# A conditioned transformer block on one core: inputs loaded earlier, weights split in halves, a new order of the tiles, and filler products ahead of the first tile's transposes

## The reference

```
def _tc_rmsnorm(x, t, gw, gb, bw, bb):
    g = (t @ gw.T + gb)[:, None, :]
    b = (t @ bw.T + bb)[:, None, :]
    inv_rms = jax.lax.rsqrt(jnp.mean(x * x, axis=-1, keepdims=True) + EPS)
    return g * x * inv_rms + b
...
x = x + _attention(_tc_rmsnorm(x, t, g1w, g1b, b1w, b1b), Wq, Wk, Wv, Wo)   # 16 heads of 16
return x + _swiglu(_tc_rmsnorm(x, t, g2w, g2b, b2w, b2b), gate_w, hid_w, out_w)   # 1024 hidden
```

## Time and profile before

| | |
|---|---|
| median of 3 runs | 944.69 us (942.25 to 944.82) |
| the profiled execution | 942.75 us, its span 940.5 us |
| mean granted clock of TensorE | 0.987 |
| busy in the span | PE 898.8 us, DVE 624.5, ACT 552.3, POOL 493.3 |

### The profile page before, as it was taken

The page is one execution under the profiler, slowest core; times in us unless marked ns, Lnnn a source line. Parts: engine busy times, 40 slices in busy tenths (PEclk is TensorE's granted clock), DMA queues, the critical chain, the costliest instruction groups (busy, mean ns, idle before and its releaser), DMA issues.

```text
span 940.5 us, 24138 instructions
## 1 busy us (share of the span) xinstructions
PE 898.8 (96%) x8988; PEld 771.4 (82%) x8988; DVE 624.5 (66%) x1067; ACT 552.3 (59%) x1255; POOL 493.3 (52%) x409
## 2 busy tenths in 40 slices
PE   5668999999999999999999999999999999999998
PEld 3456888978888898888888888888888888888887
DVE  3637668486866848677584867758476775857642
ACT  4456657565665756566575656657575665655541
POOL 4554637364563746456373644737365472735433
PEclk9879999999999999999999999999999999999999
DMA  5300102020110101011020101102010110200000
GB/s 194 102 24 23 35 25 57 2 56 22 45 34 22 56 0 56 22 45 34 19 59 0 56 22 45 34 5 73 0 54 24 45 34 0 56 0 23 2 23 23
DMA packets 25595, 34.06 MB, mean 36 GB/s; under 512 B 3296, under 2 KB 20896, under 8 KB 25440
## 3 DMA queue, kind: packets, MB, share of 16 engines
q1 hardware_dynamic: 25344, 33.59, 11.5%
q10 hardware_dynamic: 224, 0.10, 0.0%
HBM read 25.27 MB, written 8.42 MB: 36 GB/s over the span
## 4 chain that ended last, share of the span: by engine, by line
PE 88%; DVE 4%; ACT 4%; issue 3%; DMA 1%; POOL 0%; ACTq 0%; SPq 0%; DVEq 0%
PE ps L1084 9%; PE ps L1086 9%; PE ps L1085 9%; PE ps L1220 7%; PE ps L1226 7%; PE ps L1221 6%; PE ps L1236 6%; PE ps L1239 6%; PE ps L1237 6%; PE ps L1192 5%; PE ps L1207 4%; PE ps L1112 4%; PE ps L1113 3%; PE ps L1115 3%; PE ps L1182 2%
## 5 line engine op out<-in xcount | busy, mean ns | idle before, releaser
L293 POOL TENSOR_TENSOR h_lo<-h,h_hi 128x512 fp32r<-128x512 f32 x128 | 164.1, 1291 | 178.7 <-ACT h_hi L522 178.7
L299 POOL TENSOR_TENSOR probs<-probs,recip 128x512 f32<-128x512 f32 x128 | 131.8, 1045 | 48.6 <-DVE recip L829 47.1
L840 DVE SCALAR_TENSOR_TENSOR shared<-shared,ps 128x512 f32<-128x512 f32 x128 | 86.8, 678 | 97.1 <-ACT shared L517 97.1
L1084 PE MATMUL ps<-out_w_hi,h_hi 128*128 128x256 f32 x512 | 144.9, 283 | 0.0
L1086 PE MATMUL ps<-out_w_hi,h_lo 128*128 128x256 f32 x512 | 144.7, 283 | 0.0
L1085 PE MATMUL ps<-out_w_lo,h_hi 128*128 128x256 f32 x512 | 144.2, 282 | 0.0
L1220 PE MATMUL ps<-xn_hi,gate_w_hi 128*128 128x512 f32 x256 | 106.2, 415 | 2.5 <-ACT xn_hi L488 2.0
L847 DVE SCALAR_TENSOR_TENSOR h<-shared,ps 128x512 f32<-128x512 f32 x128 | 87.4, 683 | 28.9 <-PE ps L1239 23.5
L517 ACT ACTIVATE shared<-ps 128x512 f32<-128x512 f32 x128 | 76.1, 595 | 51.6 <-PE ps L1226 51.6
L532 ACT COPY probsT<-ps 128x512 f32<-128x512 f32 x128 | 69.2, 590 | 63.1 <-PE ps L1192 63.1
L1236 PE MATMUL ps<-xn_hi,hid_w_hi 128*128 128x512 f32 x256 | 106.2, 415 | 0.0
(11 more groups left out here) (92 smaller groups left out, 2008.0 us busy)
## 6 DMA issues: line engine op xcount, KB each, us to landing
x_in<-in_x SPq DMA_DIRECT2D x16, 512.0 KB, 3.4
xT_in<-in_xT SPq DMA_DIRECT2D x16, 512.0 KB, 3.3
out<-result SPq DMA_DIRECT2D x15, 512.0 KB, 3.0
inv_all<-inv_rows SPq DMA_DIRECT2D x15, 256.0 KB, 3.9
shared<-in_attT SPq DMA_DIRECT2D x1, 1024.0 KB, 7.8
shared<-in_gateT SPq DMA_DIRECT2D x1, 1024.0 KB, 9.7
shared<-in_hidT SPq DMA_DIRECT2D x1, 1024.0 KB, 4.8
shared<-in_outT SPq DMA_DIRECT2D x1, 1024.0 KB, 5.8
```

The costliest lines, as they stand in the source:

```text
L293: nc.gpsimd.tensor_tensor(h_lo[:, j % KEPT, :], h[:, j % 2, :], h_hi[:, j % KEPT, :].bitcast(F32), ALU.subtract).then_inc(h_lo_done, 1)
L299: nc.gpsimd.tensor_tensor(own, own, recip[:, p % TOGETHER, :].unsqueeze(2).to_broadcast([P, SEQS, L]), ALU.mult).then_inc(divided, 1)
L1084: nc.tensor.matmul(dst, a_hi, b_hi, start=first, stop=False, skip_group_check=skip)
```

## The change

The change has five parts.

1. *Early input.* SP loads tile 1's input right after the weights have been issued and, in later tiles, at the start of the iteration. x_res is loaded from memory by a transfer of its own; `keep_input` on ScalarE is gone.
2. *Head.* PE spreads the factors before the first gains. VectorE writes the scaled first tile into PSUM (`PAIR + 2` and `PAIR + 3`) and does the whole first norm of tile 0 from there (`whole_norm1`), both channel halves, instead of a half on VectorE and a half on ScalarE.
3. *Weights in halves.* Gate, hidden and out weights are split in two pieces each; `w_split` counts to 8 instead of 5.
4. *New orders* for all tiles on all engines. In the first tile ScalarE also makes the second keys and queries, VectorE the first queries.
5. *Fillers.* In the first tile each `transpose_probs` is preceded by four filler products into its own bank, once `shift` has used the scores there.

```diff
@@ SP
+            sp.wait_ge(ms1_done, 1)
+            sp.dma_start(x_in[:, :, :], x_t[1]).then_inc(x_loaded, 16)
+            sp.wait_ge(scaled1, 1)
+            sp.dma_start(xT_in[:, :, :], xT[1]).then_inc(xT_loaded, 16)
+            sp.dma_start(x_res[:, :, :], x_t[0]).then_inc(x_res_loaded, 16)
...
+                elif attend:
+                    if ahead:
+                        sp.wait_ge(ms1_done, t + 1)
+                        sp.dma_start(x_in[:, :, :], x_t[t + 1]).then_inc(x_loaded, 16)
+                        sp.wait_ge(scaled1, t + 1)
+                        sp.dma_start(xT_in[:, :, :], xT[t + 1]).then_inc(xT_loaded, 16)
+                    sp.wait_ge(sum_done, t)
+                    sp.dma_start(x_res[:, :, :], x_t[t]).then_inc(x_res_loaded, 16)
+                    if finish:
+                        sp.wait_ge(result_done, 2 * (t - 1))
+                        sp.dma_start(out_t[t - 2], result[:, :, :]).then_inc(stored, 16)
+                    if ahead:
+                        next_factors(t)
@@ GpSimd, first tile
+                next_inverse(t)
+                low_gate_weights(0)
+                low_gate_weights(1)
                 divide(t, 0)
-                low_hid_weights()
-                next_inverse(t)
                 divide(t, 1)
+                scale_rows(t + 1)
                 divide(t, 2)
                 divide(t, 3)
+                low_hid_weights(0)
                 divide(t, 4)
+                low_norm1(t + 1, 0)
+                low_norm1(t + 1, 1)
                 divide(t, 5)
                 divide(t, 6)
-                scale_rows(t + 1)
                 divide(t, 7)
-                low_norm1(t + 1, 0)
-                low_norm1(t + 1, 1)
-                low_out_weights()
+                low_hid_weights(1)
+                low_out_weights(0)
+                low_out_weights(1)
@@ VectorE, head
-                nc.vector.tensor_tensor(xn1[:, :, :], xT_in[:, :, :],
+                nc.vector.tensor_tensor(ps[:, PAIR + 2:PAIR + 4, :], xT_in[:, :, :],
...
+            def whole_norm1():
+                for c in range(CH):
+                    scaled = ps[:, PAIR + 2 + c, :].rearrange("p (b q) -> p b q", q=L)
+                    last = nc.vector.tensor_tensor(scaled, scaled, of_sequences(0, c, 0), ALU.mult)
+                last.then_inc(gained1, 1)
+                dve.wait_ge(gained1, 1)
+                for c in range(CH):
+                    nc.vector.tensor_tensor(xn1[:, c, :].rearrange("p (b q) -> p b q", q=L),
+                                            ps[:, PAIR + 2 + c, :].rearrange("p (b q) -> p b q", q=L),
+                                            of_sequences(1, c, 0), ALU.add).then_inc((xn1_first, xn1_second)[c], 1)
@@ VectorE, steady tile, middle
                 silu(u, 4)
+                first_norm1(t + 1)
                 hidden(u, 4)
                 row_maxima(t, 4)
...
-                first_norm1(t + 1)
@@ PE
             def transpose_probs(t, p):
+                if alone(t):
+                    pe.wait_ge(shift_done, p + 1)
+                    keep_clock_up(FILL_STEP, bank_of(t, p))
                 pe.wait_ge(divided, PAIRS * t + p + 1)
...
+            pe.wait_ge(consts_in, 16)
+            spread_factors()
             pe.wait_ge(mod_in, 2 * 16)
             gains_and_shifts(0)
-            pe.wait_ge(consts_in, 16)
-            spread_factors()
@@ PE, steady tile, first half after the change
                 gate(u, 0)
                 scores(t, 0)
                 hid(u, 0)
                 gate(u, 1)
                 hid(u, 1)
                 gate(u, 2)
+                hid(u, 2)
                 down(u, 0)
-                hid(u, 2)
                 gate(u, 3)
+                hid(u, 3)
+                down(u, 1)
+                gate(u, 4)
                 transpose_probs(t, 0)
                 transpose_probs(t, 1)
-                hid(u, 3)
-                gate(u, 4)
                 transpose_probs(t, 2)
                 transpose_probs(t, 3)
                 hid(u, 4)
                 scores(t, 1)
                 values_probs(t, 0)
                 gate(u, 5)
...
```

More of the change, by code:

```diff
@@ L439, in _, with high_weights @@
             act.wait_ge(table_loaded, 1)
-            def high_weights(n, landed, count, hi, piece):
-                act.wait_ge(landed, count)
-                nc.scalar.copy(hi, raw[:, piece, :]).then_inc(w_hi_done, 1)
+            def high_weights(landed, hi, piece, half):
+                act.wait_ge(landed, 16)
+                nc.scalar.copy(hi, raw[:, piece, half * HID:(half + 1) * HID]).then_inc(w_hi_done, 1)
             def mean_squares(u, src, ready, counts, trash, read, ms, ms_done):
@@ L490, in first_keys @@
             def first_keys(u):
+                if alone(u):
+                    act.wait_ge(consts_in, 16)
                 act.wait_ge(k_mm, CH * u + 1)
@@ L539, in _, with high_att_weights, high_gate_weights, other_keys @@
             squares1(0)
-            act.wait_ge(att_w_in, 16)
-            for part in range(2):
+            def high_att_weights(part):
+                act.wait_ge(att_w_in, 16)
                 nc.scalar.copy(att_w_hi[:, 2 * part:2 * part + 2, :, :].rearrange("p m c n -> p (m c n)"),
                                raw[:, 0, part * HID:(part + 1) * HID]).then_inc(w_hi_done, 1)
-            act.wait_ge(consts_in, 16)
-            act.wait_ge(mod_done, 2 * CH)
-            second_norm1(0)
+            high_att_weights(0)
             for c in range(CH):
                 high_norm1(0, c)
[L549 to L557, removed]
+            high_att_weights(1)
+            def high_gate_weights(half):
+                high_weights(gate_w_in, gate_w_hi[:, half, :], 1, half)
+            def other_keys(u):
+                act.wait_ge(k_mm, CH)
+                for head in range(2):
+                    last = nc.scalar.activation(keys[:, 1, :, head, :],
+                                                ps[:, k_bank(u, 1), :].rearrange("p (b q) -> p b q", q=L), ACT.Copy,
+                                                scale=head_mask[:, head:head + 1])
+                last.then_inc(keys1_done, 1)
+            def other_queries(u):
+                act.wait_ge(q_mm, CH)
+                nc.scalar.copy(queries[:, 1, :], ps[:, q_bank(u, 1), :]).then_inc(queries1_done, 1)
+            def high_hid_weights(half):
+                high_weights(hid_w_in, hid_w_hi[:, half, :], 0, half)
+            def high_out_weights(half):
+                high_weights(out_w_in, out_w_hi[:, KEPT * half:KEPT * half + KEPT, :].rearrange("p j n -> p (j n)"),
+                             1, half)
             def scale_second(t):
@@ L946, in steady_tile @@
                 row_maxima(t, 0)
+                shift(t, 0)
+                hidden(u, 0)
                 row_maxima(t, 1)
+                shift(t, 1)
+                silu(u, 1)
                 row_maxima(t, 2)
-                hidden(u, 0)
-                shift(t, 0)
-                silu(u, 1)
-                shift(t, 1)
                 hidden(u, 1)
-                reciprocals(t, 0)
                 row_maxima(t, 3)
+                shift(t, 2)
                 silu(u, 2)
-                reciprocals(t, 1)
-                shift(t, 2)
                 hidden(u, 2)
                 shift(t, 3)
+                reciprocals(t, 0)
+                reciprocals(t, 1)
                 reciprocals(t, 2)
@@ L1021, in last_tile @@
                 shift(t, 4)
+                hidden(u, 4)
                 shift(t, 5)
@@ L1024, in last_tile @@
                 reciprocals(t, 4)
-                silu(u, 4)
                 row_maxima(t, 7)
-                hidden(u, 4)
+                shift(t, 6)
+                low_attention(t, 0)
+                silu(u, 5)
+                shift(t, 7)
                 reciprocals(t, 5)
-                shift(t, 6)
-                shift(t, 7)
-                low_attention(t, 0)
                 reciprocals(t, 6)
-                silu(u, 5)
                 reciprocals(t, 7)
@@ L1127, in project_q @@
                     pe.wait_ge(xn1_lo_done, CH)
-                    wait(pe, q_act_done, c)
+                    wait(pe, queries0_done, c)
                 else:
@@ L1413, in after_last @@
                 gate(u, 2)
-                down(u, 0)
                 hid(u, 2, False)
                 gate(u, 3)
+                down(u, 0)
                 hid(u, 3, False)
@@ L1424, in after_last @@
                 gate(u, 6)
+                down(u, 3)
                 hid(u, 6, False)
-                down(u, 3)
                 gate(u, 7)
```

312 lines of the change are left out of this document (156 added, 156 removed).

## The result

The changed kernel takes 969.76 us (median of 4 runs, 967.97 to 971.37); the kernel before, run beside it, 943.73 (942.25 to 944.82). The ratio is 1.0278, with a 95% interval of 1.0266 to 1.0291: slower by 26 us, where 968 us was forecast.

What follows compares the result with a forecast made beforehand. PE was taken to bound the kernel, with 88% of the chain and almost no slack in steady tiles. 942.75 - 11 (start) + 30.8 (hold) + 5.5 (clock) = 968 us; own range 955 to 980, 8-in-10 range 942 to 985.

Steps and rivals of the forecast that it cites:

- the hold: Steady tile: next norm's gain and shift, each held behind a GpSimd low part, delay hidden 4; PE waits 2.2 us, 30.8 in all.
- the clock's term: Steady tiles: PE's gap lowers its granted clock in some tiles, about 1.6 us a fall, 5.5 us in all.
- nothing later in the tile has slack: Steady tile: PE's 2.2 us wait at the values product is not given back later in the tile.
- a VectorE operation of this form stands until GpSimd's current instruction ends and then takes 0.55: Norm operations with two SBUF operands: each ends 0.55 us after GpSimd's current instruction; unheld they would take 0.7 each.
- (a): Rival, steady tile: GpSimd is not inside a low part when the norm comes, so nothing is held; 932 us, chance 0.17.
- (b): Rival, steady tile: only one of the two norm operations is held, PE waits 0.95 us, no fall; 945 us, chance 0.08.
- I take a quarter of the tiles: Steady tiles: between none and fourteen clock falls, 0 to 22 us, a quarter of the tiles was assumed, 5.5 us.
- (c): Rival: the clock falls in every steady tile, sixteen transposes standing in one run ahead of the gap; 985 us, chance 0.1.
- The start: Head and first tile: earlier projections and the new order gain 11 us, bounds 8 and 13.
- (d): Rival: the first tile gains nothing, fillers at the lower clock and out weights taking it back; 979 us, chance 0.05.
- within 1.5 us either way: Tail: the new orders of the last two iterations were put at nothing, within 1.5 us either way.
- less about 0.15 for transposes that now stand in one run: Steady tile: joining transposes in one run brings PE to its values product about 0.15 us earlier, at 266.55.

Runs made afterwards that it cites:

- e2: Changed kernel with GpSimd's low part 3 of each steady tile waiting until the next tile's norm is done; 946.74 us, ratio 1.0036.
- e3: Changed kernel with GpSimd's low parts 2 and 3 of each steady tile both waiting until the next tile's norm is done; 967.93 us, ratio 1.0268.
- e1: Changed kernel with VectorE's hidden 4 put ahead of the next tile's norm in the steady tile; 933.61 us, ratio 0.9901.
- e4: Changed kernel with eight filler products on PE ahead of the first values product of each of the fourteen steady tiles; 958.53 us, ratio 1.0158.
- e6: e1 with ScalarE's two copies of the high out weights moved right behind the first tile's last exponential; 931.74 us, ratio 0.9868.
- e8: e6 with fillers ahead of only the first five groups of transposes in the first tile, none ahead of the last three; 929.53 us, ratio 0.9851.

## Why the prediction was right, step by step

The time (968 against 969.76) and its main mechanism, the hold, were right. That the time came within 2 us is in part luck: the clock's term was less than half of what it cost, and errors the other way nearly made up for it. Of the terms:

- **The hold, 30.8 us forecast, 28.6 measured.** Laid on the scaling's end, hidden 4 was forecast to end 4.35 us later (264.4 to 268.75) and PE to arrive 2.15 later; they came 4.06 (93.29) and 2.08 (91.31) later. (By its own terms, 265.3 + 1.44 - 0.15, PE's arrival is 266.59 and not 266.55, which makes nothing of the result.) Of the gaps' 28.6 us 14 x 1.94 = 27.2 lengthen the tiles: about 0.1 us a tile was given back, against "nothing later in the tile has slack". The cause is shown: with GpSimd still during one of the two operations that one falls to 0.69 (e2), with GpSimd still during both, both do (e3), and without the two ahead of hidden 4 the wait is gone (e1). The step "a VectorE operation of this form stands until GpSimd's current instruction ends and then takes 0.55" measured 0.55 again, at the gain (91.02 behind 90.47) and at the shift (92.69 behind 92.14). What the sum did not name is that hidden 4 also waits for low part 2; there that costs nothing, since low part 2 ends before the gain does, and e3 shows what it costs elsewhere. What the rule leaves open, who goes next, went as forecast: the shift stood behind low part 3. The Trainium skill, SBUF — State Buffer, section "SBUF: two separate sides", calls the shared port pair an exclusive lock for a whole instruction; the 1.76 and 1.64 us beside two low parts, and the 0.69 without, agree. Rivals (a) and (b), in which none or one is held, did not come; (b) was in effect built as e2, which took 946.74 where (b) had 945.
- **The clock, 5.5 us forecast, 12.1 measured.** The step that failed in size is "I take a quarter of the tiles": it was eight of fourteen. A fall cost 1.51 us, where 1.6 was taken. e4 confirms the sum at 11 us. Why eight tiles fall and six don't, the runs do not show: their gaps are alike (2.01 to 2.13 us in the six, 2.02 to 2.05 in the eight), and in the eight the fall comes at different times behind the gap, since the same product takes anything from 1.45 to 1.94 us. Rival (c), the fall in every tile, did not come; that the run of sixteen transposes alone lowers the clock falls with e1. The Trainium skill, TensorE: Matmul & The Clock Gate, "Part 4: PE-mode transpose", by which transposes count less for the clock than products, is neither shown nor refuted by that: the run of sixteen with products on both sides stays at 1.00.
- **The start, 11 us forecast, 9.8 measured.** The head was right (projections at 16.44, forecast 16.5; second scores at 29.99, forecast 30), and so was its ground: the two gains from PSUM took 1.30 us together from 12.29 on, though GpSimd cut weights until 13.25. The last values product came 1.5 us later than forecast (51.83 against 50.3), the projection out at 55.91 against 54.4, and the residual's end 1.7 later (60.69 against 59.0). The fillers ahead of the last three groups took 3.65 us, from their starts to the transposes behind them, in place of 2.85: the first group stood in a stretch at the lower level (granted clock 0.50 from 45 to 47 us), and so did part of the query projection ahead of it. That they and the out weights lie on the path was forecast; e6 and e8 show both in the trace. The transposes behind the residual waited 2.33 instead of 1.18 and ran for 1.45 instead of 1.09 (granted clock 0.89 from 64 to 65 us, 0.50 in the next), which takes back some of the gain. Rival (d), no gain in the start, did not come.
- **Not counted.** The tail gained 2.3 us ("within 1.5 us either way"). And "less about 0.15 for transposes that now stand in one run" is not there: from its start to the next product the run of sixteen took 1.66 us (253.32 to 254.98 in e1), while twice the run of eight of before took 1.58. e1's steady tile is 55.40 where before it was 55.17; of these 0.23 us the run of sixteen makes 0.08, and a new run of four another 0.14 (0.49 in e1, 0.35 in the changed kernel): with the run of twelve, 1.23, e1's transposes take 3.38 us a tile, and four runs of eight took 3.16.

The errors nearly cancel: -3.6 in the hold, +6.6 in the clock, +1.2 in the start, -2.3 in the tail, sum +1.9. The span grew by 27.2 us where 25.3 were forecast, the same 1.9; by the times it is 969.54 - 968 = 1.5.

## What to carry to other kernels

Before moving a VectorE operation with two SBUF operands ahead of something that TensorE waits for, look which GpSimd instructions run beside its new place: each such operation costs the rest of GpSimd's current instruction, and two in a row can be held twice. Where TensorE is saturated, a gap costs more than its length: here 2.04 us cost 39.3 / 14 = 2.8 on average, through the clock. A semaphore that keeps the two engines apart pays only if what stands behind the wait isn't needed by the same path (e3 against e2).

## What the runs showed of the hardware that was not expected

- VectorE and GpSimd alternated when both had work of this kind ready: low part, gain, low part, shift. The two low parts took 2.98 us together there, and 2.49 and 2.52 where no operation of VectorE came between (e3, e1).
- A gap of the same 2.0 us lowered the granted clock to 0.50 in eight of fourteen tiles (seven in e3) and not in the others; gaps of 1.2 us (e2) in none.
- A handoff between two instructions that depend on each other took 0.15 us on VectorE itself and 0.16 to 0.24 between VectorE and GpSimd (e3), so three of them in a row are worth most of one 0.69 us operation.
